# Marks of columns for four token blocks in one F16 operation, with the tokens' numbers in the marks of places

## The reference, cut to what matters

```
logits = xf @ Wr
topk_p, topk_i = jax.lax.top_k(softmax(logits), TOP_K)          # TOP_K = 2 of 8 experts
gate = zeros((N, N_EXPERTS)).at[arange(N)[:, None], topk_i].add(topk_p / sum(topk_p))
for e in range(N_EXPERTS):
    routed += (new_gelu(xf @ Wfc[e] + bfc[e]) @ Wproj[e] + bproj[e]) * gate[:, e:e + 1]
x = x + 0.5 * (shared + routed)
```

## Time and profile before

| | before |
|---|---|
| median of 3 runs | 1185.23 us (1183.57 to 1189.68) |
| the profiled execution | 1186.23 us, its span 1184.5 us |
| PE, DVE busy | 90%, 71% of the span |
| marks on DVE, both MoEs | 128 of `marks_hi`, 38.6 us; 128 of `marks_lo`, 31.7 us |
| marks made, first MoE | 46.3 to 82.2 us |
| marks made, second MoE | 661.1 to 687.5 us |
| granted PE clock, mean | 0.954 |

### The profile page before, as it was taken

The page is one execution under the profiler, slowest core; times in us unless marked ns, Lnnn a source line. Parts: engine busy times, 40 slices in busy tenths (PEclk is TensorE's granted clock), DMA queues, the critical chain, the costliest instruction groups (busy, mean ns, idle before and its releaser), DMA issues.

```text
span 1184.5 us, 16414 instructions
## 1 busy us (share of the span) xinstructions
PE 1066.8 (90%) x4800; PEld 731.3 (62%) x4800; DVE 840.4 (71%) x2362; ACT 669.8 (57%) x1265; POOL 683.2 (58%) x786
## 2 busy tenths in 40 slices
PE   6779999998989999999979979999967678999996
PEld 6336778875657677667745448888734445555553
DVE  6785787767867887787765967777762676767661
ACT  2336767765566676667543338777744445545533
POOL 4006556637998888877662046666465665754330
PEclk9989999999999999999987989999996888989998
DMA  8666667741000000000001036877510000000000
GB/s 270 240 261 210 213 214 246 239 127 29 14 14 13 14 14 12 15 5 1 1 19 54 1 117 213 252 241 241 162 53 19 16 16 25 25 12 10 10 18 18
DMA packets 67976, 108.81 MB, mean 92 GB/s; under 512 B 8336, under 2 KB 46224, under 8 KB 67856
## 3 DMA queue, kind: packets, MB, share of 16 engines
q1 hardware_dynamic: 57904, 87.30, 22.1%
q0 software_dynamic: 9984, 20.47, 6.8%
HBM read 81.00 MB, written 28.57 MB: 93 GB/s over the span
## 4 chain that ended last, share of the span: by engine, by line
PE 58%; POOL 17%; DVE 11%; issue 6%; ACT 5%; DMA 2%; POOLq 0%; SPq 0%; DVEq 0%; ACTq 0%
PE bank L193 7%; PE bank L426 3%; PE bank L427 3%; PE bank L428 3%; PE bank L443 3%; PE bank L445 3%; PE bank L444 3%; POOL wr L642 3%; PE bank L1071 3%; PE bank L1077 3%; PE bank L1596 3%; PE bank L424 2%; PE bank L1111 2%; PE bank L1617 2%; POOL got L642 2%
## 5 line engine op out<-in xcount | busy, mean ns | idle before, releaser
L586 POOL DMA_INDIRECT spare_all<-xs,list_row x184 | 191.7, 1042 | 210.9 <-DVE list_row L724 107.4
L781 DVE TENSOR_TENSOR hid_lo<-hid,hid_hi 128x512 fp32r<-128x512 f32 x184 | 127.0, 692 | 75.0 <-ACT hid L528 73.4
L528 ACT ACTIVATE hid<-bank,b_up_of 128x512 f32<-128x512 f32 x184 | 125.6, 684 | 6.5 <-PE bank L428 1.2
L527 ACT ACTIVATE hid_hi<-bank,b_up_of 128x512 fp32r<-128x512 f32 x138 | 95.3, 690 | 47.7 <-PE bank L428 35.2
L642 POOL DMA_INDIRECT got<-ys,y_slots x80 | 87.3, 1091 | 51.0 <-issue 40.7
L193 PEld LDWEIGHTS bank<-ident,spare_all 128*128 128x128 f32 x504 | 64.8, 150 | 78.0 <-issue 57.6
L193 PE MATMUL bank<-ident,spare_all 128*128 128x128 f32 x504 | 82.1, 289 | 26.1 <-DVE spare_all L372 18.0
L1190 ACT ACTIVATE gate_b<-bank,head_rstd 128x128 f32<-128x128 f32 x256 | 73.0, 370 | 55.7 <-POOL head_rstd L1297 55.2
L528 ACT ACTIVATE hid<-bank,cols_sb 128x512 f32<-128x512 f32 x64 | 43.9, 687 | 88.4 <-PE bank L424 79.4
L426 PE MATMUL bank<-xh,wr 128*128 128x512 f32 x184 | 82.4, 448 | 3.5 <-DVE xl L774 3.5
L1863 DVE TENSOR_TENSOR gate_b<-bank,spare_all 128x512 f32<-128x512 f32 x64 | 43.1, 687 | 50.2 <-PE bank L1617 48.0
(11 more groups left out here) (291 smaller groups left out, 2749.0 us busy)
## 6 DMA issues: line engine op xcount, KB each, us to landing
wr<-wq SPq DMA_DIRECT2D x92, 512.0 KB, 4.7
ys<-spare_all SPq DMA_DIRECT2D x46, 256.0 KB, 5.3
wq<-wr SPq DMA_DIRECT2D x16, 512.0 KB, 5.7
got<-in_w_mlp SPq DMA_DIRECT2D x8, 512.0 KB, 5.9
xs<-spare_all SPq DMA_DIRECT2D x16, 256.0 KB, 2.3
spare_all<-xs,list_row POOLq DMA_INDIRECT x184, 3.7
out_x<-X SPq DMA_DIRECT2D x8, 256.0 KB, 2.3
ys<-in_x SPq DMA_DIRECT2D x1, 1792.0 KB, 10.5
```

What stands on the lines that cost most here:

```text
L528: nc.scalar.activation(hid[:, n % HC], bank[up_bank(n)][:], ACT.Gelu_apprx_tanh, bias=bias).then_inc(s["gelu_done"], 1)
L586: g.indirect_dma_start(out=xin[:, j % XIN, b], out_offset=None, in_=xs, in_offset=bass.IndirectOffsetOnAxis(ap=list_row[:, n:n + 1], axis=0))\
L781: v.tensor_tensor(hid_lo[:, q], hid[:, n % HC], hid_hi[:, q].bitcast(F32), ALU.subtract).then_inc(s["lo_done"], 1)
```

## The change

`marks_hi` of a unit is made by one comparison of F16 tables instead of four: `column_by_block` holds 0 to 91, each four times side by side, and is compared with the four blocks' column numbers, read again for every column. The result lies column by column with the four blocks inside, so it holds 1 or 0, and a matmul reads one block's 92 columns at a step of four elements. The token's number, formerly multiplied into `marks_hi`, is multiplied into `marks_lo`, so those four operations now have two scalars per row instead of one. `column_by_block` is made once, in the first MoE's setup; `spot_hi` is copied to F16 once in each MoE.

```
-        marks_hi = sb("marks_hi", [P, 2, TB, COLUMNS], F16)
+        marks_hi = sb("marks_hi", [P, 2, COLUMNS, TB], F16)
+        column_by_block = sb("column_by_block", [P, COLUMNS, TB], F16)
+        spot_hi16 = sb("spot_hi16", [P, TOP * BLOCKS], F16)
...
-                    ins = nc.tensor.matmul(bank[6][:, TW - COLUMNS:], marks_lo[:, u % 2, m], marks_hi[:, u % 2, m],
+                    ins = nc.tensor.matmul(bank[6][:, TW - COLUMNS:], marks_lo[:, u % 2, m], marks_hi[:, u % 2, :, m],
...
                 steps.link(v.tensor_scalar(spot_hi[:], spot_n[:], -12582912.0, None, ALU.add))
+                steps.done(v.tensor_copy(spot_hi16[:], spot_hi[:]))
                 steps.link(v.scalar_tensor_tensor(spot_lo[:], spot_hi[:], -float(P), spot_f[:], ALU.mult, ALU.add))
...
-                for m in range(TB):
-                    at = u * TB + m
-                    v.tensor_scalar(marks_lo[:, u % 2, m], column_no16[:], spot_lo[:, at:at + 1], None, ALU.is_equal)
-                    ins = v.tensor_scalar(marks_hi[:, u % 2, m], column_no16[:, 0:COLUMNS], spot_hi[:, at:at + 1],
-                                          token_no[:, at % BLOCKS:at % BLOCKS + 1], ALU.is_equal, ALU.mult)
+                at = u * TB
+                by_block = spot_hi16[:, at:at + TB].unsqueeze(1).broadcast_to([P, COLUMNS, TB])
+                v.tensor_tensor(marks_hi[:, u % 2], column_by_block[:], by_block, ALU.is_equal)
+                for n in range(at, at + TB):
+                    ins = v.tensor_scalar(marks_lo[:, u % 2, n - at], column_no16[:], spot_lo[:, n:n + 1],
+                                          token_no[:, n % BLOCKS:n % BLOCKS + 1], ALU.is_equal, ALU.mult)
                 ins.then_inc(s["marked"], 1)
...
                 v.tensor_copy(column_no16[:], column_no[:])
+                v.tensor_copy(column_by_block[:], column_no[:, 0:COLUMNS].unsqueeze(2).broadcast_to([P, COLUMNS, TB]))
```

## The result

The changed kernel takes 1184.06 us (median of 20 runs, 1181.55 to 1189.8), the kernel before 1187.51 us (median of 20 runs beside it, 1183.14 to 1192.89). The ratio is 0.9966 with a 95% interval of 0.9952 to 0.9981, so the change wins 4.0 us (2.3 to 5.7). In a second set of runs, with the kernel unaltered, the ratio is 0.9947 (0.9916 to 0.9977). The forecast was 1179 us, a ratio to its base of 0.9947: a gain of 6.2 us. The sign was right, most of the gain's mechanism too, and the size too large; 1184.06 lies at the upper end of the range, just outside it. The forecast's ratio lies just outside the first set's interval and inside the second's, so the size of the gain is known only to some 2 us. Of the 5.1 us between forecast and median, 2.3 us are the base itself (1185.23 us for three runs, 1187.51 for the twenty), and the rest is a smaller gain.

The account below looks back on a forecast made before the run. PE, busy 90% of the span, was taken as the bound, with DVE's marks mattering only where PE waits. First MoE 4.1 plus second 2.4 gave 6.5 us off 1186.2, 1179.7, forecast 1179 us after median adjustment; range 1176 to 1184.

Parts of the forecast that it names:

- The first rival: DVE's two-input comparison runs at the f32 rate, a unit takes 1.34 us; gain 3.8 us, 1181.5 us; chance 0.15.
- A cost that I put at nothing: PE's matmuls reading the moving table at a step of four: 0 to 0.47 us a unit, taken as nothing.
- Break-even: Extra PE cost a unit that would cancel the gain: 6.5 / 23 = 0.28 us, 71 ns a matmul.
- the third rival: PE's matmuls with gaps become the bound; at the high end 10.8 us lost, 1189.5 us; chance 0.05 from breaking even up.
- DVE's worst unit: Marks of a unit on DVE take 1.45 us instead of 1.15; only 1.2 us won, the range's slow end.
- First MoE: 4.1 us forecast: Middle of 2.8 us (all bound by weight loads) and 5.2 us (shorter marks 3.55 plus clock 1.67).
- the 1.67 of the forecast: Time lost to PE's low clock at 78.60 to 82.24 us in the first MoE, expected to go more often than not.
- the criteria I had set for being wrong: First MoE: `keep_rows` starting less than 3 us earlier, or the second list turned less than 2.8 us earlier.
- this fall: PE's granted clock dropping to 0.75 in the window 80 to 84 us of the first MoE, costing 1.67 us.
- Second MoE: 2.4 us forecast: All of PE's waits for marks there, 2.4 us, go, and no more, since PE is then without a gap.
- Weight loads hold it: First MoE: low clock stays and the second list waits for weight loads; gain 5.2 us, 1180 us; chance 0.15.

Follow-up runs that it names:

- the token's number moved: Kernel before the change, with only the token's number moved from the marks of columns to the marks of places, nothing batched: 1187.73 us, ratio 0.9985.
- only the layout: Kernel before the change, with `marks_hi` laid column by column, still written by four operations, and read by matmuls with gaps: 1192.85 us, ratio 1.0034.
- the second MoE alone: Changed kernel with the new marks in the second MoE only, the first marking as before: 1186.41 us, ratio 0.9996.
- block by block: Changed kernel with its one comparison laid out by block, one element repeated for 92 columns, matmuls reading neighbouring columns: 1182.37 us, ratio 0.9965.
- a step of eight: Changed kernel with four unused elements after each column's four blocks, so matmuls read every eighth F16 element: 1189.52 us, ratio 1.0003.
- two comparisons: Changed kernel with `marks_hi` made by two 184-column operations, matmuls reading at a step of two: 1181.55 us, ratio 0.9973.
- the first MoE alone: Changed kernel with the new marks in the first MoE only, the second marking as before: 1184.42 us, ratio 0.9979.
- before's marks: Kernel before the change, with only DVE's order altered in the first MoE, marks made ahead of the weight split: 1181.66 us, ratio 0.9959.

## Why the prediction was right on DVE and wrong on PE

**DVE, right.** 344 ns (350), 307 ns (309), a unit 1.15 us, and the halving of a column's price by F16 also with two inputs. The sentence on the Trainium skill ("VectorE: DVE Perf Modes", section "The perf-mode tier table") held: 16 bits gave the two-input operation its factor of two, in this layout. The first rival, f32 rate, is excluded here, and shown to be real for another layout: with one repeated element the same 368 columns took 534 ns.

**A cost that I put at nothing: the step that failed.** The matmul's moving table at a step of four F16 elements costs 80 ns for 92 columns, not 43: 0.15 us a unit. I had kept a range of 0 to 0.47 us more a unit (43 to 160 ns a matmul) and taken its low end; the measured price is a third of the way up. By the forecast's own count it is 16 units in the second MoE and 7 in the first, 3.45 us. With it the sum is 6.5 - 3.45 = 3.05 us, with the measured 4.0 (2.3 to 5.7) around it. The Trainium skill's rule of 16-byte lines and two hits on each ("Advanced Engine Details and Errata", section "Memory Cachelines"), on which the nothing leaned, does not agree: at 8 bytes two hits fall on each line, and the price is still double. The trace decides. Break-even was 0.28 us a unit, so the third rival named the right place and had the wrong size. No row of the trace before could have given it. The middle of the bounds, 0.235 us a unit, would have left 1.1 us, too little. What the forecast could have done is carry the open price in its range: the upper end, 1184, came from DVE's worst unit alone, and no term of it was PE's.

**First MoE: 4.1 us forecast.** Marks: 3.55 + 1.67 less 7 x 0.15 = 4.17 us expected with that price, 4.49 measured, and 3.85 where this MoE alone was changed; the second list 4.66 us earlier. The pieces of the 4.49: each of five cycles is 0.6 us shorter (7.26 to 6.67), 3.0 us; the last unit, read at a step of four, costs 0.15; and before had the low clock twice, from 64.96 to 68.38 us, which the forecast did not count and which lengthened a cycle by 0.13 us, and from 78.62 to 82.03, which is the rest, some 1.5 us for the 1.67 of the forecast.

```profile
66.00:68.00 2.00, 2.00 (x7) 0.88 (x6) 0.96 (x2) 1.01 (x2) 0.00 (x0) 0.50 0.35 143
```

So a third of the gain read from this pair of executions is the clock's, and hangs on where the low clock fell in each; that the 4.1 us come out so near is in part luck. Neither of the criteria I had set for being wrong (under 3 us, under 2.8 us) was met.

**The clock.** The place of the low clock changes from execution to execution. With the marks behind the split, there are two or three such stretches during the first MoE's marks in each of six executions (before, the token's number moved, only the layout, the second MoE alone, block by block, a step of eight), though not always at 78 to 82 us: with the token's number moved they lie at 49.14 to 55.96 and 66.20 to 69.61. In the four executions where DVE's unit takes at most 1.22 us and PE reads at a step of four or less there are none, none, one (two comparisons) and two (the first MoE alone), none of them at 78 to 82 us. With the marks ahead of the split there is none in any of four executions, before's marks among them. So the forecast that this fall goes "more often than not, but it may also come elsewhere" was met, but that the shorter units are the cause is not shown: it is a count of one execution a kernel, two for the changed one.

**Second MoE: 2.4 us forecast, 0.30 measured.** The waits went, as said. "And no more, since PE is then without a gap" was the sentence that should have made me price PE: without gaps, every cost on PE is on the path. 16 x 0.15 = 2.4 us used up the gain. With a step of two it is there, 2.59 us.

**Weight loads hold it.** Not in the changed kernel. The loads moved by less than forecast, 2.12 us for 2.84 (the first at 89.46 us, 91.58 in the earlier trace rows; the fill of `ys` by 1.84), and the second list still came 4.66 us earlier, so the list did not hang on them.

```profile
89.46 0.27 SPq L891 DMA_DIRECT2D wr<-wq  x1
```

It came true one step further, when the marks ended another 7 us earlier.

## What to carry to other kernels

When a change relays a tile so that its producer gets cheaper, price the consumer's read as carefully: here DVE won 0.36 us a unit and PE lost 0.15, and where PE was the bound nothing was left. A price that no row shows belongs in the forecast's range and not at its low end. Where a stall's removal leaves an engine with no gaps, every cost that was put at nothing on that engine comes due there. And read the chain of waits for its order before making its pieces faster: making the marks ahead of the split won by itself as much (4.9 us by its ratio) as the change (4.0 us), and both together about 11.

## What the runs showed of the hardware

- A matmul of 92 F16 columns at full clock takes, from start to start, 43 ns with its moving table at a step of one or two elements, 80 ns at four and 160 ns at eight. From a step of four to one of eight it goes with the bytes passed over, 92 x 8 = 736 bytes in 80 ns and 1472 in 160, 9.2 bytes a ns; by that rate a step of two would be 40 ns (an estimate), under the 43 ns that neighbouring columns take. Steps beyond eight were not run.
- A two-input F16 comparison of 368 columns takes 344 ns when its second input is four neighbouring elements read again and again, and 534 ns when it is one element repeated. With two neighbouring elements read again, 184 columns take 247 ns: 97 ns less for 184 columns fewer, 0.53 ns a column, so a run of two is enough.
- A one-input F16 operation that writes 92 columns at a step of four lasts 383 ns in place of 301, but its start-to-start distance grows only from 0.215 to 0.24 us: most of the difference overlaps with the next instruction. A two-input one that writes four elements and skips four lasts 347 ns in place of 344.
